# Sink-window attention with int8 feed-forward on Trainium2: rows of a step ordered by query, heads within

## What is computed

```python
h = layernorm(x)
q = (h @ wq.T)  # 16 heads of 128;  k, v: 4 heads of 128, each serves 4 query heads
scores = einsum('bhtd,bhsd->bhts', q, k_full) / sqrt(128)
mask = (k <= q) & ((k < 4) | (k >= q - 31))      # 4 sinks and a window of 32
attn = masked_softmax(scores, mask)
x = x + (einsum('bhts,bhsd->bhtd', attn, v_full) -> [b, t, 2048]) @ wo.T
h = layernorm(x)
xq, wq8 = int8 quantised rows of h and of weight
x = x + (xq @ wq8.T) * x_scale * w_scale + bias
```

## Time and profile before

| | |
|---|---|
| median of 3 runs | 634.7 us (633.99 to 635.71) |
| profiled execution, own time | 634.63 us |
| its span, first to last instruction | 632.8 us |
| mean granted TensorE clock | 0.987 |
| TensorE, VectorE busy | 599.3 us (95%), 544.8 us (86%) |
| ScalarE, GpSimd busy | 399.7 us (63%), 307.8 us (49%) |

### The profile page before, as it was taken

One profiled execution on the slowest core, in us unless ns is written; L12 is line 12 of the kernel. 1 busy time (PEld: TensorE's weight loads), 2 busy tenths in 40 slices (PEclk: granted clock), 3 DMA queues, 4 the chain that ended last, 5 costly groups with the idle time before them and its releaser, 6 DMA issues.

```text
span 632.8 us, 18148 instructions
## 1 busy us (share of the span) xinstructions
PE 599.3 (95%) x7589; PEld 529.5 (84%) x7589; DVE 544.8 (86%) x1084; ACT 399.7 (63%) x631; POOL 307.8 (49%) x302
## 2 busy tenths in 40 slices
PE   5759999999999999999999999999999999999983
PEld 4547888889898988989898888989898888989872
DVE  5876899989898988989898998989898998988885
ACT  5676766566666666666666666667666666665740
POOL 1142445464565546455554646456554745535440
PEclk9989999999999999999999999999999999999996
DMA  9931401213040311203040221304030120304000
GB/s 295 352 103 20 116 1 49 55 35 85 3 117 2 86 34 46 73 15 105 1 120 2 67 52 37 83 9 112 3 96 24 53 68 20 99 1 118 3 18 34
DMA packets 33841, 41.31 MB, mean 65 GB/s; under 512 B 3936, under 2 KB 24416, under 8 KB 33760
## 3 DMA queue, kind: packets, MB, share of 16 engines
q1 hardware_dynamic: 33616, 40.02, 22.9%
q10 hardware_dynamic: 144, 0.13, 0.1%
HBM read 10.26 MB, written 4.19 MB: 23 GB/s over the span
## 4 chain that ended last, share of the span: by engine, by line
PE 87%; DVE 7%; ACT 3%; issue 1%; POOL 1%; DMA 1%; POOLq 0%; SPq 0%; ACTq 0%
PE ps L551 26%; PE ps L429 25%; PE ps L456 7%; PE ps L396 7%; PE ps L405 6%; PE ps L512 5%; PE ps L533 4%; PE ps L534 4%; PE ps L384 1%; PE ps L578 1%; DVE WoT L1008 1%; DVE Qs L892 1%; PE ps L566 1%; PE ps L336 1%; DMA X<-in_L_attn_x 1%
## 5 line engine op out<-in xcount | busy, mean ns | idle before, releaser
L429 PE MATMUL ps<-xT,WqT 128*128 128x256 f16 x1536 | 178.2, 273 | 2.0 <-DVE WqT L1008 1.3
L551 PE MATMUL ps<-WoT,pool 128*128 128x256 f16 x1536 | 178.0, 273 | 0.2 <-DVE pool L916 0.2
L429 PEld LDWEIGHTS ps<-xT,WqT 128*128 128x128 f16 x1536 | 147.0, 98 | 19.1 <-issue 3.0
L551 PEld LDWEIGHTS ps<-WoT,pool 128*128 128x128 f16 x1536 | 147.5, 98 | 16.4 <-DVE pool L916 0.3
L1203 POOL TENSOR_TENSOR small<-E,rr 128x576 f32<-128x576 f32 x63 | 72.6, 1152 | 99.8 <-DVE rr L911 99.8
L775 ACT ACTIVATE pool<-ps 128x512 f16<-128x512 f32 x128 | 69.5, 595 | 81.7 <-PE ps L534 81.6
L1209 POOL TENSOR_TENSOR PP<-small,PP 128x576 f16<-128x576 f32 x63 | 80.9, 1284 | 68.2 <-ACT PP L768 68.2
L735 ACT ACTIVATE Qs<-ps 128x576 f16<-128x576 f32 x128 | 82.4, 644 | 43.6 <-PE ps L429 43.6
L1195 POOL TENSOR_TENSOR Sm<-Sm,mx 128x576 f32<-128x576 f32 x64 | 73.7, 1152 | 54.2 <-DVE mx L902 52.9
L892 DVE TENSOR_TENSOR Qs<-ps,Qs 128x576 f16<-128x576 f32 x128 | 92.6, 724 | 3.2 <-ACT Qs L735 3.0
L916 DVE SCALAR_TENSOR_TENSOR pool<-ps,pool 128x512 f16<-128x512 f32 x128 | 81.8, 680 | 0.8 <-ACT pool L775 0.8
(11 more groups left out here) (110 smaller groups left out, 888.0 us busy)
## 6 DMA issues: line engine op xcount, KB each, us to landing
VW<-Vn SPq DMA_DIRECT2D x48, 120.0 KB
big<-Vn SPq DMA_DIRECT2D x48, 120.0 KB
X<-in_L_attn_x SPq DMA_DIRECT2D x16, 256.0 KB, 7.7
VW<-VW SPq DMA_DIRECT2D x16, 256.0 KB, 3.2
big<-big SPq DMA_DIRECT2D x16, 256.0 KB, 3.4
out<-pool SPq DMA_DIRECT2D x15, 256.0 KB, 3.6
big<-in_L_attn_wq SPq DMA_DIRECT2D x4, 512.0 KB, 7.6
pool<-in_L_attn_wo SPq DMA_DIRECT2D x4, 512.0 KB, 9.1
```

Of the source, the lines that this page charges most:

```text
L429: a = pe.matmul(banks[BANK_Q[f]][:, j * 256:j * 256 + 256], WqT[:, k, wl, h * 128:h * 128 + 128], xT[:, b % 2, k, xl, :], start=(n == 1), ...
L551: a = pe.matmul(banks[BANK_OUT][:, t * 256:t * 256 + 256], OT[:, p, ol, h, t * 128:t * 128 + 128], WoT[:, 4 * g + h, wl, :], start=first, ...
```

## The change

The rows of a tile are ordered by query from last to first, with the four heads within: row 4 * (31 - i) + h in place of 32 * h + i. Qs is written so, with a step of -4 elements along the queries. The mask is permuted alike. The last 16 rows of a tile are then its first four queries, which tiles 1 to 8 don't use: `p_transpose` takes rows 0 to 111 there (128 in tile 0), in ascending order of tiles, and writes each tile's columns as one run. The PSUM bank and PT then hold 4 * (255 - q) + h. `pv` reads and writes single runs. `o_view` reads the two output banks with a step of -4 along the queries; OT keeps its layout.

```diff
         def q_views(p, f):
             src = bass.AP(ps, 512 * BANK_Q[f], [[4096, 128], [256, 2], [STEP, NT], [1, 32]])
-            dst = [bass.AP(Qs, ((p * 2 + l) * NT * 128) + 64 * f, [[4 * NT * 128, 128], [32, 2], [128, NT], [1, 32]])
+
+            dst = [bass.AP(Qs, (p * 2 + l) * NT * 128 + 4 * 31 + 2 * f, [[4 * NT * 128, 128], [1, 2], [128, NT], [-4, 32]])
                    for l in range(2)]
...
         def o_view(j):
-            return banks[BANK_O[j]][:, :].rearrange("p (h q) -> p h q", h=4), slice(128 * j, 128 * j + 128)
+            return bass.AP(ps, 512 * BANK_O[j] + 4 * 127, [[4096, 128], [1, 4], [-4, 128]]), slice(128 * j, 128 * j + 128)
...
-                v = half(pt_bank(u), F16).rearrange("p (h q) -> p h q", h=4)
-                for s in reversed(range(NT)):
-                    a = pe.transpose(v[:, :, STEP * s:STEP * s + 32], PP[:, p, s].rearrange("p l k -> p (l k)"), idh[:, :])
+                v = half(pt_bank(u), F16)
+                for s in range(NT):
+
+                    n, at = 4 * (q0_of(s + 1) - q0_of(s)), 4 * (T - q0_of(s + 1))
+                    a = pe.transpose(v[:, at:at + n], PP[0:n, p, s].rearrange("p l k -> p (l k)"), idh[0:n, 0:n])
                 a.then_inc(pt_ps, 1)
...
-                    o = banks[BANK_O[j]][:, :].rearrange("p (h q) -> p h q", h=4)[:, :, c0 - 128 * j:c1 - 128 * j]
-                    pt = PT[:, u % 2].rearrange("p (h q) -> p h q", h=4)[:, :, c0:c1]
+                    o = banks[BANK_O[j]][:, 4 * (128 * j + 128 - c1):4 * (128 * j + 128 - c0)]
+                    pt = PT[:, u % 2, 4 * (T - c1):4 * (T - c0)]
...
                 if k <= q and (c < 4 or (k >= 4 and k >= q - WIN + 1)):
-                    m[i::32, s, c] = 0.0
+                    m[4 * (31 - i):4 * (31 - i) + 4, s, c] = 0.0
```

## The result

The changed kernel takes 683.57 us in the median of four runs (682.99 to 685.27), against 635.21 us for the kernel before on the same chip. The ratio is 1.0768, with a 95% interval of 1.0748 to 1.0787: 48 us or 7.7% slower, where 631.3 us and a range of 630 to 648 us had been forecast.

What follows compares the result with a forecast made beforehand. TensorE's issued columns were taken as the bound. From 634.63 us, 3.3 came off for transposes and 0 was added for loads, pieces, order, mask and stepped accesses (covered up to 0.75 us a step): 631.3 us, range 630 to 648.

Steps and rivals of the forecast that it cites:

- What bounds the kernel: Steady part: TensorE issues columns without a gap, 40.00 of 40 us busy; other engines count only once TensorE waits.
- The transposes' gain: TensorE: eight of nine transposes a step stream 112 columns instead of 128, 6.7 ns saved each, 3.3 us taken.
- rivals 4 and 5: 4: transposes' load over 112 partitions becomes visible, 656.3 us, chance 0.04; 5: transposes not paced by columns, 634.6 us, 0.02.
- Products and transposes in one piece: TensorE: transpose outputs and product columns as one piece instead of four per-head pieces; column counts unchanged, 0.
- stepped PSUM reads: OT copies L775 (ScalarE) and L916 (VectorE) read PSUM in 16-byte steps; taken as 0, upper bound +425 and +533 ns.
- rival 1: PSUM read element by element at half rate, VectorE +1.07 us a step: 653.6 us, chance 0.10.
- Stepped accesses to Qs: Q copies L735 (ScalarE) and L892 (VectorE) step f16 by 8 bytes; taken as 0, upper bound +478 and +600 ns.
- the sink copies: L883 and L722, writing f16 runs of 4 elements with hops between; nearest trace rows, read as hops costing nothing.
- Rival 2: Qs written and read in 8-byte steps at half rate, VectorE +1.20 us a step: 661.6 us, chance 0.06.
- The cover: VectorE's waits for scores and exponentials, 48.3 us or 0.75 us a step, were to absorb longer stepped copies.
- has more room: ScalarE: 0.68 us idle before each step's first Qs copy and 0.77 us after the PT copy may absorb longer copies.
- estimate of 678 us: By the skill's 1.73 ns a column, L892 and L916 would grow by about 389 and 346 ns; total about 678 us.

Runs made afterwards that it cites:

- kernel with pairs: Changed kernel, same Qs layout, but the Q copies walk query outside and two heads inside, writing aligned runs of 2 f16: 632.56 us, ratio 0.9969.
- kernel with plain Qs copies: Changed kernel with the Q copies writing Qs head by head again in unbroken runs of 32, high and low part: 632.82 us, ratio 0.9962.
- three kernels that have the gain without the loss: Kernel with plain Qs copies (632.82 us), kernel with pairs (632.56 us), and the kernel before with 112 rows laid out head by head (632.71 us).

## Why the prediction was wrong, point by point

- *What bounds the kernel* was right: TensorE's columns, seen again at 480.00 of 480 us in the kernel with pairs. (The "35.7 to 35.8" given for VectorE are the values of the weight loads, the column beside it; VectorE's own in the windows of the earlier trace rows are 35.3 to 36.0. Nothing hangs on it.)
- *The transposes' gain* was right in mechanism. The chain of the kernel with plain Qs copies gives 0.45 us for the nine at L515, where it gave 0.50 at L512:

```profile
296.19 0.45 PE ps L515 x9
```

  So the load over 112 partitions stays hidden (rivals 4 and 5 fall). Over 60 steps the transposes of the kernel before and of the kernel with pairs lie so:

```profile
58.78 0.67 PE L512 MATMUL ps<-idh,PP 128*128 128x128 f16 x9
...
599.15 0.67 PE L512 MATMUL ps<-idh,PP 128*128 128x128 f16 x9
```

```profile
58.33 0.61 PE L515 MATMUL ps<-idh,PP 128*128 128x128 f16 x9
...
595.95 0.61 PE L515 MATMUL ps<-idh,PP 128*128 128x128 f16 x9
```

  That is 540.37 against 537.62 us, 2.75 us where 60 x 8 x 6.7 ns = 3.2 us were summed. By the ratios of the three kernels that have the gain without the loss it is 2.0 to 2.5 us over the whole run, each within about 1 us. So the 3.3 us of the sum were somewhat too much.
- *Products and transposes in one piece* at 0, *stepped PSUM reads* at 0: right, though the larger chance among the penalties had gone to PSUM (rival 1, 0.10), which cost nothing in any form tried. What "PSUM — Partial Sum Buffer" of the Trainium skill says in Specifications (TRN2) of non-contiguous patterns is about matmuls; for reads by VectorE and ScalarE the runs show no price at 16, 32, 64 bytes (691 and 597 ns for 512 elements) or 1 KB (757 and 650 ns for 576).
- *Stepped accesses to Qs* at 0 is the step that failed: they cost 674 ns a copy on VectorE and 780 ns on ScalarE. The ends were named; the choice of the lower one rested on the sink copies, from which the prediction took that "a hop after each 8 bytes is free". They hop only after four elements have filled two whole words. The stepped copy hops after every element and leaves half of each word unwritten, and that difference decides. The upper end was too low as well, 600 ns for VectorE and 478 for ScalarE, since the price is not a multiple of the engine's own element time but one of the target's lines, the same on both engines. Rival 2 named the cause, at 661.6 us and a chance of 0.06; with VectorE's measured 1.35 us a step its own sum gives 634.6 + (1.35 - 0.75) x 60 = 671 us. (The sums of rivals 1 and 2 leave out the 3.3 us that the transposes give back; with them it is 667 us.)
- *The cover*: VectorE's 0.75 us a step is confirmed, by 634.23 us at one stepped copy and by 662.9 us at two, where the sum by cover had put 667; that it was the waits that covered is shown for about half of the time, as said above. ScalarE "has more room" was wrong: its room was read as idle time ahead of single instructions in one step, but the chain through VectorE and POOL comes back to it, in the step shown here one with batch statistics. That made 10 to 11 us of one stepped copy a step and 17.8 us of two, and is what lifts the result from VectorE's share (662.9 us) to 683.6.
- "SBUF — State Buffer" of the Trainium skill, in its note on cachelines, lets bf16 step within a 16-byte line for free. f16 reads at 8 bytes agree (757 ns), at 16 bytes they cost 1159 ns; lone f16 writes at 8 bytes (1432 ns) don't agree, and the measurement decides. "Vector Engine (DVE) Microarchitecture Reference" of the Trainium skill, in its paragraph on the SBUF access granule, has 1.73 ns a column for one source that hops 4 KiB at every element; a source alone in its line at 16 bytes comes near it, (1159 - 147) / 576 = 1.76 ns. The same paragraph's demand for runs of two adjacent words does not show in f32 written at 8 bytes (757 ns on VectorE). The prediction's estimate of 678 us carried that SBUF figure over to L916, whose stepped source lies in PSUM, where the step costs nothing (680 ns before and after).

## What to carry to other kernels

When a copy to f16 is to interleave something, make the innermost loop of its access pattern write aligned pairs, and let the source hop instead: in PSUM the hops tried here, 16, 32 and 64 bytes and 1 KB, were free. A row of the trace bounds a new access pattern only if it matches in what one access fills, not just in how far it jumps. And an engine at 63% is not covered by its idle time where a late result returns to it through the queues of two others: follow its consumers to the end before costing a longer instruction at nothing.

## What the hardware showed that was not expected

An f16 written alone to SBUF, its word not filled by its neighbour in the walk, costs about 4.2 to 4.5 ns for each visit to a 16-byte line, on VectorE and ScalarE alike: 576 elements take 797 and 802 ns at 4 bytes, 1432 and 1442 at 8, 2702 and 2714 at 16. Runs of three (1009 ns) and misaligned pairs (1432 ns) pay it per line too. Aligned pairs at 8, 16 or 32 bytes from pair to pair don't on VectorE (757 to 758 ns); on ScalarE they take 650, 675 and 685 ns. All of these copies read f32 from PSUM and write f16; other 16-bit types weren't tried. That the price belongs to the line is worked out from these durations; what the memory does in that time, no run shows.
